# Windowed attention layers on one core: scores and values in 64-row halves of TensorE, and a new order of five engines

## The reference

```
for i in range(DEPTH):                                   # 6
    x = attn_layer(shift_tokens(x), Wqkv[i], q_scale[i], k_scale[i], Wo[i]) + x
    x = ffn_layer(shift_tokens(x), ln_g[i], ln_b[i], W1[i], b1[i], W2[i], b2[i]) + x

shift_tokens(t): the second half of the features is taken from the token before
attn_layer: q, k, v = x @ Wqkv (128 -> 3 x 1024, 16 heads of 64); q, k normed, scaled and rotated;
            windows of 32 tokens; a query sees its own window and the one before (mask);
            sim = q.k * 8, softmax, times v; then @ Wo (1024 -> 128)
ffn_layer:  layer norm, h = xn @ W1 + b1 (128 -> 2 x 341), a * gelu(gate) @ W2 + b2
```

## Time and profile before

| | us |
|---|---|
| median of 3 runs | 4062.19 (4061.96 to 4063.85) |
| the profiled execution | 4059.29 |
| its span on the core | 4057.3 |
| TensorE busy | 3896.8 (96%) |
| ScalarE busy | 3727.0 (92%) |
| VectorE busy | 3473.4 (86%) |
| GpSimd busy | 2329.7 (57%) |

### The profile page before, as it was taken

How to read it: one execution, slowest core, us unless ns; L and a number is a source line. 1 busy time by engine, 2 the same in 40 slices (tenths; PEclk the granted TensorE clock), 3 DMA queues, 4 the chain that set the end, 5 groups by cost and what they waited for, 6 DMA issues and landing times. The chain is left out here.

```text
span 4057.3 us, 122291 instructions
## 1 busy us (share of the span) xinstructions
PE 3896.8 (96%) x43124; PEld 2851.0 (70%) x43124; DVE 3473.4 (86%) x8234; ACT 3727.0 (92%) x7250; POOL 2329.7 (57%) x2687
## 2 busy tenths in 40 slices
PE   4999999997999999999999999999999999999995
PEld 2555555554777777777777777777777777777774
DVE  4888888867888888888888888888888888888884
ACT  4888988867999999999999999999999999999995
POOL 4000000017777777777777777777777777777773
PEclk7899999988999999999999999999999999999997
DMA  6777877741111111111111111111111111111111
GB/s 185 240 248 237 249 242 242 244 151 47 40 45 44 49 45 40 45 44 49 45 40 45 45 49 44 40 45 44 50 45 40 45 46 48 44 40 45 48 47 54
DMA packets 249788, 348.35 MB, mean 86 GB/s; under 512 B 45104, under 2 KB 206364, under 8 KB 249116
## 3 DMA queue, kind: packets, MB, share of 16 engines
q1 hardware_dynamic: 249244, 340.94, 28.1%
HBM read 151.07 MB, written 82.85 MB: 58 GB/s over the span
## 5 line engine op out<-in xcount | busy, mean ns | idle before, releaser
L1490 PE MATMUL la_ps<-la_Wqkv,la_xsT 128*128 128x512 f32 x2304 | 1174.3, 603 | 6.2 <-DVE X L1186 6.2
L1186 DVE TENSOR_TENSOR X<-la_ps,la_tab 128x1024 f32<-128x1024 f32 x768 | 938.0, 1221 | 102.5 <-ACT la_sq L1334 96.2
L1116 POOL TENSOR_TENSOR la_rt<-X 128x512 f32<-128x512 f32 x384 | 496.1, 1292 | 586.9 <-PE la_ps L1505 435.2
L1133 POOL TENSOR_TENSOR la_rt<-la_rt,la_rn 128x1024 f32<-128x1024 f32 x384 | 722.5, 1902 | 29.8 <-POOL la_rn L1128 3.5
L1195 DVE TENSOR_REDUCE la_ssum<-la_sq 128x8 f32<-128x512 f32 x768 | 510.9, 665 | 0.0
L1334 ACT ACTIVATE la_sq<-la_ps 128x512 f32<-128x512 f32 x768 | 464.8, 605 | 35.6 <-PE la_ps L1490 30.9
L1117 POOL TENSOR_TENSOR la_rt<-X 128x512 f32<-128x512 f32 x384 | 495.8, 1291 | 0.0
L1521 PEld LDWEIGHTS la_ps<-la_kT,la_qB 128*64 128x64 f32 x12288 | 390.4, 138 | 85.1 <-issue 73.7
L1490 PEld LDWEIGHTS la_ps<-la_Wqkv,la_xsT 128*128 128x128 f32 x2304 | 362.6, 191 | 120.9 <-issue 75.2
L532 POOL COPY at_vh<-V 128x64 f32 (+1 forms) x64 | 15.2, 241 | 748.6 <-PE at_ps L743 748.5
L1521 PE MATMUL la_ps<-la_kT,la_qB 128*64 128x64 f32 x12288 | 432.9, 223 | 0.0
(11 more groups left out here) (205 smaller groups left out, 8868.3 us busy)
## 6 DMA issues: line engine op xcount, KB each, us to landing
at_band<-skew_scratch SPq DMA_DIRECT2D x64, 1536.0 KB, 7.3
la_vs<-la_v SPq DMA_DIRECT2D x192, 384.0 KB, 3.5
skew_scratch<-at_R SPq DMA_DIRECT2D x64, 1024.0 KB, 9.5
la_vs<-la_v SPq DMA_DIRECT2D x192, 128.0 KB, 3.4
la_Wqkv<-in_wqkv SPq DMA_DIRECT2D x28, 384.0 KB, 5.2
at_qh<-qt_scratch SPq DMA_DIRECT2D x64, 144.0 KB
at_kh<-kt_scratch SPq DMA_DIRECT2D x64, 144.0 KB
la_W<-in_L_ffn_W SPq DMA_DIRECT2D x24, 341.0 KB, 5.0
```

Of the source, the lines that this page charges most:

```text
L1116: e.tensor_tensor(dst[:, :, 0, :], c[:, :, 0, :], s[:, :, 1, :], ALU.add)
L1133: e.tensor_tensor(heads(rt, w), heads(rt, w), wide(rn[:, w * H:(w + 1) * H], D), ALU.mult)\
L1186: e.tensor_tensor(dst.rearrange("p f (h d) -> p f h d", d=D), ps[:, c % 2, :].rearrange("p (h d) -> p h d", d=D).unsqueeze(1).to_broadcast ...
L1490: e.matmul(ps[:, c % 2, :], xsT[:, m * P:(m + 1) * P], Wqkv[:, ds(layer(n) % 2, 1), c * 512:(c + 1) * 512], start=True, stop=True)\
```

## The change

Scores: `qB` with its zeros is replaced by `qT`, plain q. Each matmul takes one head: 64 rows of q and k, 32 columns of weights (32 queries), 64 streamed (keys). 64 matmuls a tile, no longer in two halves; the head's parity chooses row half and bank (BANK_S + par). Values: likewise `pT` for `pB`, 64 matmuls of 64 rows (one window pair `wl` of keys), 64 columns of weights, 32 streamed, into bank OUT[wl]. `q_turned` and `p_turned` become one copy each per bank; the memsets of `qB` and `pB` go. Loads of tables are now placed by `table_of`, where the set changes. All five bodies have a new order. That of the steps spoken of below, before and after, lag in brackets:

- TensorE before: qkv 1 (2), turn_x (0), hidden 2 (7), turn_p 0, 1 (5), qkv 2 (2), back_out (7), scores 0 (4), values 0 (5), scores 1 (4), values 1 (5), qkv 3 (2), turn_y (6), qkv 4 (2), turn_q 0, 1 (3), hidden 0 (6), out_proj (5), qkv 5 (2), hidden 1 (6), qkv 0 (1), turn_k 0, 1 (3)
- TensorE after: out_proj (6), turn_p 0 (5), qkv 2 (2), turn_x (0), hidden 0 (7), scores (4), turn_p 1 (5), qkv 3 (2), back_out (8), hidden 1 (7), values (5), qkv 4, 5 (2), hidden 2 (7), turn_q 0, 1 (3), qkv 0 (1), turn_y (6), qkv 1 (1), turn_k 0, 1 (3)
- ScalarE after: x_turned (0), squared 3 (2), gelu 1 (7), exp 0 (4), o_out 0, 1 (5), v_out 4 (2), one (6), exp 1 (4), v_out 5 (2), q_turned 0, 1 (3), y_turned (6), squared 0, 1 (1), k_turned 0, masked 0, k_turned 1 (3), guess (2), masked 1 (3), gelu 0 (6), gelu 2 (7), squared 2 (1), p_turned 0, 1 (4)

The diff, cut:

```diff
 RING_V, RING_T = 4, 4
-DEEPEST = 7
+DEEPEST = 8
 BY_DVE = (2, 3, 6, 8, 10)
...
-        N_IN, SET = 7, 7
+        TURNED_Q, TURNED_K, TURNED_P, OUT = (4, 5), (4, 5), (4, 5), (4, 5)
+        N_IN, SET = 7, 6
 
         def layer(n):
...
             def body(t):
                 for n, m in t.back(4):
+                    y_shifted(n, m)
+                for n, m in t.back(5):
+                    next_layer(n, m)
+                for n, m in t.back(4):
                     w1_in(n, m)
-                    next_layer(n, m)
-                for n, m in t.back(3):
-                    y_shifted(n, m)
                 for n, m in t.back(0):
                     v_shifted(n, m)
...
                 for n, m in t.back(3):
-                    added(n, m, 1)
-                for n, m in t.back(4):
-                    carried(n, m)
+                    scaled(n, m, 0)
+                for n, m in t.back(6):
+                    root(n, m)
                 for n, m in t.back(0):
                     table(n, m)
-                for n, m in t.back(6):
-                    root(n, m)
-                for n, m in t.back(3):
-                    newton(n, m)
-                    scaled(n, m, 0)
-                    scaled(n, m, 1)
-                for n, m in t.back(2):
-                    added(n, m, 0)
                 for n, m in t.back(7):
                     with_b2(n, m)
+                for n, m in t.back(3):
+                    scaled(n, m, 1)
+                for n, m in t.back(2):
+                    added(n, m, 0)
+                    added(n, m, 1)
+                for n, m in t.back(3):
+                    carried(n, m)
+                for n, m in t.back(2):
+                    newton(n, m)
...
-                    clipped(n, m)
+                for n, m in t.back(6):
+                    if m % 2:
+                        gated(n, m, 2)
+                for n, m in t.back(0):
+                    turned(n, m, 2)
+                for n, m in t.back(2):
+                    largest(n, m, 0)
+                    below(n, m, 0)
+                for n, m in t.back(4):
+                    stats(n, m)
+                for n, m in t.back(0):
...
+            loaded = []
+
+            def table_of(name):
+                if loaded[-1:] != [name]:
+                    e.preload_act_table_set(name)
+                    loaded.append(name)
+
...
                 e.wait_ge(Tq_mm.sem, Tq_mm.v(n, u + 1))
-                e.wait_ge(S_mm.sem, S_mm.v(n - 1, u + 1))
-                e.activation(qB[0:D, 4 * u:4 * u + 4, :, 0, :], src[0:D], ACT.Copy)
-                e.activation(qB[D:P, 4 * u:4 * u + 4, :, 1, :], src[D:P], ACT.Copy).then_inc(Tq_ev.sem, 1)
+                e.wait_ge(S_mm.sem, S_mm.v(n - 1))
+                e.activation(qT[:, 4 * u:4 * u + 4, :], ps[:, TURNED_Q[u], :].rearrange("p (j t) -> p j t", j=4),
+                             ACT.Copy).then_inc(Tq_ev.sem, 1)
 
             def k_turned(n, m, u):
...
 
             def exp(n, m, h):
+                table_of(LN_AND_EXP)
                 e.wait_ge(sub_ev.sem, sub_ev.v(n, h + 1))
                 e.activation(ps[:, BANK_S + h, :], ps[:, BANK_S + h, :], ACT.Exp).then_inc(ex_ev.sem, 1)
...
-            def o_out(n, m, h):
-                e.wait_ge(pv_mm.sem, pv_mm.v(n, h + 1))
+                e.wait_ge(pv_mm.sem, pv_mm.v(n - 1))
+                e.activation(pT[:, 4 * h:4 * h + 4, :], ps[:, TURNED_P[h], :].rearrange("p (j c) -> p j c", j=4),
+                             ACT.Copy).then_inc(pt_ev.sem, 1)
+
+            def o_out(n, m, l):
+                e.wait_ge(pv_mm.sem, pv_mm.v(n))
                 e.wait_ge(wo_mm.sem, wo_mm.v(n - 1))
-                e.activation(oT[:, 4 * h:4 * h + 4, :], ps[:, OUT[h], :].rearrange("p (j t) -> p j t", j=4),
+                e.activation(oT[:, :, l * D:(l + 1) * D], ps[:, OUT[l], :].rearrange("p (j t) -> p j t", j=8),
...
-                for j in range(4):
+                e.wait_ge(mk_ev.sem, mk_ev.v(n))
+                for c in range(4):
                     for wl in range(2):
-                        for g in range(2):
-                            w, col = g + 2 * wl, j * P + wl * D
-                            at = m % RING_V * P + w * WIN
-                            mm = e.matmul(bank[g * D:(g + 1) * D, col:col + D], qB[:, 4 * h + j, w, :, :],
-                                          kT[:, 4 * h + j, at:at + 2 * WIN], start=False, stop=True,
-                                          skip_group_check=True)
-                mm.then_inc(S_mm.sem, 1)
+                        for jj in range(2):
+                            for g in range(2):
+                                w, at = g + 2 * wl, m % RING_V * P + (g + 2 * wl) * WIN
+                                to = slice((2 * g + jj) * WIN, (2 * g + jj + 1) * WIN)
+                                col = c * P + wl * D
+                                for par in range(2):
+                                    of = slice(par * D, (par + 1) * D)
+                                    mm = e.matmul(ps[to, BANK_S + par, col:col + D], qT[of, 2 * c + jj, w * WIN:(w + 1) * WIN],
+                                                  kT[of, 2 * c + jj, at:at + 2 * WIN], start=False, stop=True,
+                                                  skip_group_check=True)
+                mm.then_inc(S_mm.sem, 2)
 
...
-
-                e.wait_ge(pt_ev.sem, pt_ev.v(n, h + 1))
+            def values(n, m):
+
+                e.wait_ge(pt_ev.sem, pt_ev.v(n))
                 e.wait_ge(v_ev.sem, v_ev.v(n))
                 e.wait_ge(vs_in[m % 2].sem, vs_in[m % 2].v(n // 2))
-                for j in range(4):
-                    pair = 4 * h + j
+                for pair in range(H // 2):
+                    c, jj = pair // 2, pair % 2
                     for g in range(2):
+                        keys = (vs[:, m % 2, :], v[:, m % RING_V, :])[g]
+                        at, to = (2 * g + jj) * WIN, pair * D + g * WIN
                         for par in range(2):
-                            keys = (vs[:, m % 2, :], v[:, m % RING_V, :])[g]
                             head, rows = (2 * pair + par) * D, slice(par * D, (par + 1) * D)
-                            to = ps[rows, OUT[h], j * P:(j + 1) * P].rearrange("p (l g q) -> p l g q", l=2, g=2)
-                            mm = e.matmul(to[:, :, g, :], keys[:, head:head + D], pB[:, pair, 2 * g + par, :, :],
-                                          start=True, stop=True, skip_group_check=True)
-                mm.then_inc(pv_mm.sem, 1)
+                            for wl in range(2):
+                                of = slice(wl * D, (wl + 1) * D)
+                                mm = e.matmul(ps[rows, OUT[wl], to:to + WIN], keys[of, head:head + D],
+                                              pT[of, 4 * par + c, at:at + WIN], start=True, stop=True, skip_group_check=True)
+                mm.then_inc(pv_mm.sem, 2)
...
             def body(t):
-                for n, m in t.back(2):
-                    qkv(n, m, 1)
+                for n, m in t.back(6):
+                    e.wait_ge(nT_ev.sem, nT_ev.v(n - 1))
+                    e.wait_ge(xT_ev.sem, xT_ev.v(upto(n + 5)))
+                    e.wait_ge(y_ev.sem, y_ev.v(n - 1))
+                    out_proj(n, m)
+                for n, m in t.back(5):
+                    e.wait_ge(Tk_ev.sem, Tk_ev.v(upto(n + 1), 1))
+                    e.wait_ge(Tq_ev.sem, Tq_ev.v(upto(n + 1), 1))
+                    e.wait_ge(o_ev.sem, o_ev.v(n - 1, 1))
...
```

More of the change, by code:

```diff
@@ L1168, in body @@
                     added(n, m, 0)
-                for n, m in t.back(7):
-                    with_b2(n, m)
+                    added(n, m, 1)
[3 more added lines that the diff above has]
+                    newton(n, m)
             straight(e, body, TILES, TB, DEEPEST)
@@ L1301, in body @@
                         gated(n, m, 1)
-                for n, m in t.back(0):
-                    turned(n, m, 0)
-                    squares(n, m, 0)
-                for n, m in t.back(6):
-                    if m % 2:
-                        next_x(n, m)
-                for n, m in t.back(5):
-                    if m % 2:
-                        gated(n, m, 2)
-                for n, m in t.back(0):
-                    turned(n, m, 1)
-                for n, m in t.back(4):
-                    stats(n, m)
+                for n, m in t.back(2):
+                    largest(n, m, 1)
+                for n, m in t.back(4):
+                    mean_over(n, m)
+                for n, m in t.back(2):
+                    below(n, m, 1)
+                    summed(n, m, 0)
+                for n, m in t.back(0):
+                    squares(n, m, 2)
+                    squares(n, m, 3)
+                for n, m in t.back(2):
+                    summed(n, m, 1)
             straight(e, body, TILES, TB, DEEPEST)
@@ L1410, in body @@
             def body(t):
-                for n, m in t.back(4):
```

(39 more changed lines are left out.)

207 lines of the change are left out of this document (67 added, 140 removed).

## The result

The changed kernel takes 5863.69 us (median, 5860.62 to 5869.19) against 4062.19: 1.4436 times as long, 95% interval 1.4418 to 1.4454. The forecast was 5575 (5050 to 5950). The profiled execution took 5864.7 us.

What follows compares the result with a forecast made beforehand. TensorE bounds at 15.79 us a tile; a loop through SP's queue makes the round 23.85, 8.06 more for 188 tiles: 1515 us on 4057.3, with 2 around the span and 2.9 to the median, 5575 us (5050 to 5950).

Steps and rivals of the forecast that it cites:

- loss to the clock: TensorE after each pause: clock halved to 1.2 GHz for a while, costing 2.1 to 3.2 us a round, 2.3 taken.
- What bounds: Layers' stage before the change: TensorE sets the pace at 15.79 us a tile, ScalarE 0.4 us behind.
- The SP queue: SP queue: y_shifted(n) waits behind v_shifted(n+3) for values(n+1), closing a loop of one tile per round; 21.55 us at full clock.
- rival 2: Loop through SP, but the clock stays full or falls only briefly: 5145 us (5065 without the 0.4); chance 0.11.
- DMA contention: Y DMA to stats: v_shifted's 512 KB still landing in the same engines delays it 0 to 2.3 us, 0.4 taken.
- TensorE's own turn: TensorE after: scores 1.14 plus values 2.10 against 3.95 us, 0.71 a tile saved, floor 15.08; 14.16 from qkv 5 on.
- rival 3: TensorE's array: row halves take turns, 2.78 us more a round on the loop, 6100 us; chance 0.11.
- ScalarE 14.2: ScalarE after: 2.4 us less copying, 1.3 more for table loads (four in two tiles), net 14.2 us a tile.
- VectorE "keeps its work" at 14.1: VectorE after: same work in other places, busy 14.1 us a tile as before.
- It saves nothing either: Side case with y_shifted not late: the change also saves nothing, time within 0.2% (8 us); chance 0.01.
- rival 4: SP queue: y_shifted isn't late, v_shifted's wait being met before with_x(n); TensorE bounds at 15.08, 3926 us; chance 0.05.
- marks named in advance: Trace signs: round 23 to 25 us, TensorE idle 6, VectorE about 7, clock 0.8 to 0.9, scores near 1.1, values 2.1.

Runs made afterwards that it cites:

- lag 3: The changed kernel with one step of SyncE put back, y_shifted at lag 3 instead of 4: 4182.15 us, 1.0295 times the kernel before.
- y3_row0: The changed kernel with y_shifted at lag 3, scores and values issuing only the first row half's matmuls, 64 passes each instead of 128: 4075.65 us (one run).

## Why the prediction was right, and what was mis-sized

The direction, the mechanism and the range held; the time lay 289 us above the forecast. The terms of its round, measured as means over 136 rounds of the changed kernel (1500 to 5000 us):

| | predicted | measured |
|---|---|---|
| last pass of values to the first vs DMA | 0.31 | 0.33 |
| to the first Y DMA | 1.20 | 1.27 |
| Y DMA to stats | 3.58 + 0.4 | 4.40 |
| stats to qkv 5 | 1.90 | 1.93 |
| rest of TensorE's turn, full clock | 14.16 | 15.26 |
| loss to the clock | 2.3 | 2.2 |
| round | 23.85 | 25.41 |

The turn at full clock is what is left of the measured round, so the table's sum is no check by itself; but lag 3, where no clock is lost, takes 15.29 us from qkv 5 to the last pass of values. (25.41 - 15.79) x 188 = 1809 us, on 4059.3: 5868, 4 us off the result. The steps in turn:

- **What bounds.** Right: TensorE, and a gain of 0.71 could only come from there.
- **The SP queue.** Right, and shown three ways: by undoing the lag, by a third buffer with the lag kept, and by the lag alone in the old kernel. "The clock stays full" (rival 2) fell, and the price by analogy with the pauses of the earlier trace rows was good to 0.1 us, since the clock came back 4.3 us after the restart, as there (4.2). Rival 2's side figure is 5 us off: 0.4 x 188 less than 5145 is 5070, not 5065.
- **DMA contention.** 0.4 was taken for it, 0.82 measured; nearer the middle of its bounds, 0 and 2.3. In the changed kernel's own last two tiles, with no vs DMA under way, the Y DMA takes 3.60 and 3.58 us to stats.
- **TensorE's own turn: the term that was mis-sized**, by 1.1 of the 1.56 us. It came from the floor of 15.08, which lag 3 measures as 16.36. Values were right to the digit: 2.01 + 0.09 for the entry against 2.10. The rule of the Trainium skill ("TensorE: Matmul & The Clock Gate", section LDWEIGHTS) that weights cost by columns whatever the rows agrees: values gained nothing from 64 rows. Scores were put at 1.14, the array's 0.93 and 0.21 for the block, and take 1.57 with the entry, since after the first 32 passes they come 10.5 ns apart. The sum knew the array's steps only, and no scores of before were as dense: the earlier trace rows has 32 passes in 0.93 us, 29 ns each. The pauses (0.54), in which TensorE waits for its own instructions, and turn_p's wait (0.2) were missing altogether.
- **Row halves take turns** (rival 3): no, by y3_row0.
- **ScalarE 14.2** us a tile, with four table loads in two tiles: 14.17 (2338.8 us in 165 tiles of lag 3), and 276 loads in 138 tiles of the changed kernel. Right.
- **VectorE "keeps its work" at 14.1**: wrong. It is busy 15.7 with lag 3. Its work is the same, but mean_over came to stand beside GpSimd's scaled. Off the loop in the changed kernel, it costs up to 71 us once the loop is gone (0.08 of the 0.29 us a tile are pauses that may not be its doing). An order can't be priced by adding up durations from another order, where two engines share something.
- **"It saves nothing either"** (in rival 4, 0.01) was much too low as a side case: with the queue in order the change would still be 3% slower than before.

Of the marks named in advance, TensorE's pause (6.6), VectorE's (8.5 for 7), the Y DMAs 1.2 behind the vs DMAs, the clock (0.84) and values at 2.1 came as said; scores didn't.

## What to carry to other kernels

Before a step is moved in a DMA queue, look at what the step now ahead of it waits for, and whether that in turn comes later than what the moved step feeds. Two transfers with nothing in common were tied by a queue here, and one line cost 1681 us. When a matmul is cut into more and smaller ones, count instructions as well as array steps, and look at when the instruction queue's transfers land; and when orders of two engines change, look again for pairs that now run at the same moment.

## What the hardware showed

**VectorE held by GpSimd.** mean_over reads two operands from SBUF, and where it met scaled it ended 0.015 us after it (median). Of 164 cases in the run with lag 3, 92 began 0.23 to 0.68 us after scaled and took 1.53 us (median), 62 began with it or up to 0.22 later and took 1.92, and ten, which also began with it, ran first in 0.15. clipped (128x32, one input) ranged from 0.16 to 1.30; no run isolates it. `turned` and the reductions kept their durations to 3%. The Trainium skill ("SBUF — State Buffer", section Who interferes with whom) states this: an instruction of VectorE with two inputs in SBUF and one of GpSimd that reads SBUF exclude each other, and the later one waits to the end. The trace agrees.

**TensorE waits for its instructions.** In blocks of 128 dense passes TensorE stops now and then for 0.6 to 1.9 us with no semaphore in sight, 0.54 us a tile with lag 3, mostly after 90 passes and more. Half as many passes, the old form, or a split block have none or few. The page's queue of instructions moved more, before and after:

```profile
q8 instruction: 360, 5.90, 0.6%
```

```profile
q8 instruction: 551, 9.03, 0.7%
```

The 191 further transfers, of 16 KB each, go with 48160 further instructions, 252 for each; a block of 128 passes has 256, a matmul and a weight load for each pass. The trace has the time of each transfer, and these times tie the pauses to them. The pause shown above has one in it, as the queues from 3016.5 to 3020.2 us show:

```profile
q8 instruction: 1, 0.02, 2.0%
```

It ran from 3017.40 to 3018.56, and TensorE went on at 3020.09, 1.53 us after its end. With lag 3, from 1200 to 3900 us, TensorE stops 63 times for over 0.6 us without a semaphore, and all 63 stops end 1.21 to 1.60 us after the end of such a transfer, where an instant taken at random would lie so in less than 9% of cases. The same holds in every other run with such stops: 46 of 46 in the changed kernel, 62 of 62 with mean_over on GpSimd, 28 of 28 with values split, 470 of 470 over ten runs, between 1.14 and 1.66 us. The four with fewer transfers, at most 277 in such a stretch where lag 3 has 429 (the kernel before, with and without its lag changed, half the passes, and both forms as before), have no stop at all. So in a dense block TensorE can use up its instructions before the next 16 KB are in.

**A slower pace inside a block.** The shortest block of scores takes 1.27 us for 128 passes in every kernel that has it. Its first 32 passes start within 0.24 us, in four groups of eight: eight tiles of the array at once. From the 33rd to the last it is 1.0 us, 10.5 ns a pass (a matmul and a weight load). That the array's width isn't the limit is shown by the first 32; that the later passes are held by the rate at which instructions come is argued.
